# A graph network's third pass: the edge layer's first product in two PSUM banks, the adjacency windows in one

## The reference

```python
x = ln(x + L0(x))        # two max-aggregations with leaky relu: passes 1 and 2 over the edges
# L1, the third pass over the edges:
h = relu(edge_attr_17 @ W1.T + b1)          # "hidden", 96 wide, per edge
w = h @ W2.T + b2                           # "edge rows"
msg = w * x[src]                            # "message": x[src] is gathered
agg = segment_sum(msg, dst)                 # "sum"
x = ln(x + relu(x @ Ws.T + bs + agg @ Wn.T + bn))
x = ln(x + L2(x))        # two hops with a normalised adjacency matrix
x = ln(x + L3(x))        # one hop and a weight
```

## Time and profile before

| what | value |
|---|---|
| median of 3 runs | 4723.26 us (4720.13 to 4724.09) |
| the profiled execution | 4718.38 us |
| its span, first to last instruction | 4716.6 us |
| third pass, first hidden product to last message | 2561 to 3883 us |
| busy share of the span: PE, DVE, POOL, ACT | 75%, 53%, 50%, 20% |
| mean granted clock of TensorE | 0.843 |

### The profile page before, as it was taken

One profiled execution on the slowest core, in us unless ns is written; L12 is line 12 of the kernel. 1 busy time (PEld: TensorE's weight loads), 2 busy tenths in 40 slices (PEclk: granted clock), 3 DMA queues, 4 the chain that ended last, 5 costly groups with the idle time before them and its releaser, 6 DMA issues.

```text
span 4716.6 us, 64730 instructions
## 1 busy us (share of the span) xinstructions
PE 3549.1 (75%) x23472; PEld 2740.7 (58%) x23472; DVE 2500.2 (53%) x6368; ACT 929.8 (20%) x2714; POOL 2376.2 (50%) x2520
## 2 busy tenths in 40 slices
PE   3666776677647777777776676777777789999999
PEld 2444554454424544454444454555555569999999
DVE  4555666565636666666665455555555553232211
ACT  0100000000112222222222232332232230011100
POOL 5566666666466666666664566665565640000000
PEclk6788777777868888888887788878888889999999
DMA  5323232323223333333332222233333338777776
GB/s 148 100 63 73 63 73 65 72 62 73 60 66 104 97 102 98 101 102 106 97 103 67 68 78 70 76 90 93 105 105 103 103 98 267 275 255 257 257 275 241
DMA packets 192519, 555.56 MB, mean 118 GB/s; under 512 B 77782, under 2 KB 83382, under 8 KB 172662
## 3 DMA queue, kind: packets, MB, share of 16 engines
q1 hardware_dynamic: 67132, 335.46, 22.3%
q0 software_dynamic: 80432, 124.45, 12.8%
q10 hardware_dynamic: 44682, 92.08, 5.2%
HBM read 455.53 MB, written 96.37 MB: 117 GB/s over the span
## 4 chain that ended last, share of the span: by engine, by line
PE 46%; another core or an unknown queue 23%; DVE 14%; issue 9%; ACT 5%; ACTq 2%; DMA 1%; DVEq 0%; SPq 0%
PE banks L1443 17%; PE banks L1217 7%; PE banks L1173 5%; DVE scan L2293 5%; PE banks L1245 4%; DVE hot_key L2324 3%; PE banks L1170 3%; PE banks L1357 3%; PE banks L1189 3%; DVE hot_src L2326 2%; PE banks L1365 2%; ACT adj L1710 1%; DVE back L2298 1%; DVE hot_lo L1952 1%
## 5 line engine op out<-in xcount | busy, mean ns | idle before, releaser
L930 POOL DMA_INDIRECT gath<-table,ids x2496 | 2365.8, 948 | 1476.3 <-issue 687.2
L1217 PE MATMUL banks<-back 128*96 128x104 f32 (+11 forms) x6000 | 783.5, 279 | 180.3 <-issue 128.4
L1217 PEld LDWEIGHTS banks<-back 128*96 128x96 f32 x6000 | 721.5, 191 | 253.5 <-issue 185.3
L2324 DVE TENSOR_SCALAR hot_key<-banks,key_t 128x392 bf16<-128x392 int16 x1600 | 658.2, 411 | 315.2 <-remote 292.6
L1443 PE MATMUL banks<-r_parts,adj_in 128*128 128x288 bf16 x6543 | 809.6, 286 | 4.6 <-DMA adj_in<-adjacency 4.6
L1245 PE MATMUL banks<-hot_key,hot_src 128*128 128x392 bf16 x1600 | 459.1, 373 | 468.1 <-ACT adj L1710 292.5
L1443 PEld LDWEIGHTS banks<-r_parts,adj_in 128*128 128x128 bf16 x6543 | 802.4, 143 | 6.4 <-issue 4.4
L2293 DVE TENSOR_TENSOR_SCAN scan<-keep_of,scan,banks 96x512 f32<-96x512 bf16 x414 | 526.3, 1271 | 407.7 <-remote 320.5
L1245 PEld LDWEIGHTS banks<-hot_key,hot_src 128*128 128x128 bf16 x1600 | 149.3, 108 | 786.6 <-issue 726.0
L1173 PE MATMUL banks<-ea_of,w_edge_of 128*96 128x512 f32 x832 | 546.9, 742 | 18.3 <-issue 17.4
L1709 ACT ACTIVATE adj<-banks 128x160 bf16<-128x160 f32 x800 | 242.4, 303 | 1109.8 <-remote 720.3
(11 more groups left out here) (182 smaller groups left out, 2382.5 us busy)
## 6 DMA issues: line engine op xcount, KB each, us to landing
adj_in<-adjacency SPq DMA_DIRECT2D x114, 1568.0 KB, 6.5
adjacency<-adj ACTq DMA_DIRECT2D x100, 464.0 KB
gath<-table,ids POOLq DMA_INDIRECT x2496
ea_of<-in_ea_t SPq DMA_DIRECT2D x78, 512.0 KB
keep_of<-keep_max_d SPq DMA_DIRECT2D x52, 768.0 KB
adjacency<-adj ACTq DMA_DIRECT2D x100, 320.0 KB
adj_in<-adjacency SPq DMA_DIRECT2D x33, 928.0 KB, 4.8
ahead_of<-adjacency SPq DMA_DIRECT2D x33, 640.0 KB
```

What stands on the lines that cost most here:

```text
L930: pool.indirect_dma_start(gath[:, b, t, :], None, tables[p][:, :], bass.IndirectOffsetOnAxis(ap=ids[:, 1, n:n + 1], axis=0),).then_inc(s_g ...
L1217: m = pe.matmul(band_ps[g % 2][:, at:at + n], rows_in[:, q % 2, t * D:(t + 1) * D], hot_dst[:, q % 2, t, first:first + n], start=False, st ...
L2324: ve.tensor_scalar(hot_key[:, h, a, :], key_places_ps, key_t[:, 0, a, bass.ds(n, 1)], None, ALU.is_equal)
```

## The change

The hidden products of quarters 0 to 93 (`HID_PAIRED` = 94) alternate between banks 0 and 1, and each is issued in step `q-4`; `hidden(q)` then waits for the relu of quarter `q-2`. Before, all used bank 0, in step `q-3`, with a wait for the relu of `q-1`. From quarter 94 on bank, step and wait are as before. ACT reads the relu's input from the bank in question; its order of work is the same. To free bank 1, all 400 windows of the third pass now lie in bank 6: this moves 93 odd windows, those of the steps up to 93. In the second pass odd windows stay in bank 1. `hidden(1)` waits for the second pass's last window in bank 1, and the first `products_ahead` waits for the 94th relu, where it waited for bank 1's windows.

```diff
+HID_PAIRED = AHEAD_STEPS[0] // 2 * 2
...
-        hid1_ps = banks[0:D, 0, :]
+        hid2_ps = [banks[0:D, b, :] for b in (0, 1)]
...
         def window_bank(n):
-            step = (n - WINDOWS * BUILT) // 2 + 1
-            return 1 if n % 2 and step < AHEAD_STEPS[0] - 1 else 6
+            return 1 if n % 2 and n < WINDOWS * BUILT else 6
+        def hidden_bank(q):
+            return q % 2 if q < HID_PAIRED else 0
+        def hidden_step(q):
+            return q - (4 if q < HID_PAIRED else 3)
...
-                    if q >= 1:
+                    if q == 0:
+                        pe.wait_ge(s_copied[2], BANDS)
+                    elif q == 1:
+                        pe.wait_ge(s_window_out, windows_in(1, WINDOWS * NT))
+                    elif q < HID_PAIRED:
+                        pe.wait_ge(s_hid, q - 1)
+                    else:
                         pe.wait_ge(s_hid, q)
-                    else:
-                        pe.wait_ge(s_copied[2], BANDS)
-                    pe.matmul(hid1_ps, weights(2), columns, start=True, stop=True).then_inc(s_hid_ps, 1)
+                    pe.matmul(hid2_ps[hidden_bank(q)], weights(2), columns, start=True, stop=True).then_inc(s_hid_ps, 1)
...
-                            pe.wait_ge(s_window_out, windows_in(1, WINDOWS * NT))
+                            pe.wait_ge(s_hid, HID_PAIRED)
...
                 edge_rows(1)
+                hidden(3)
                 for s in range(QUARTERS + TAIL):
-                    if s + 3 < QUARTERS:
-                        hidden(s + 3)
+                    for q in (s + 3, s + 4):
+                        if q < QUARTERS and hidden_step(q) == s:
+                            hidden(q)
...
-                    act.activation(hid[0:D, q % 2, :], hid1_ps, ACT.Relu, bias=W["edge_in_b"][:, 0:1]).then_inc(s_hid, 1)
+                    act.activation(hid[0:D, q % 2, :], hid2_ps[hidden_bank(q)], ACT.Relu, bias=W["edge_in_b"][:, 0:1]).then_inc(s_hid, 1)
```

## The result

The changed kernel takes 4729.24 us (median of 16 runs), the kernel before 4723.7 us beside it (16 runs); the ratio is 1.0018, with a 95% interval of 1.0011 to 1.0024. That is some 8 us slower by the ratio and 5.5 us by the medians. One run of the changed kernel took 15243.89 us and is left out of the ratio. Predicted were 4735 us, a range of 4706 to 4752 us, and "slower by over 0.2%" as the likeliest case. The direction is right, and the time lies in the range. The likeliest case isn't shown, since 1.0018 is just under its bound and the interval lies on both sides of it.

What follows compares the result with a forecast made beforehand. POOL's gathers and pauses were taken to bound each step; one window bank would cost 12 us (between 6 and 16) and the other edits nothing, so 4723.3 + 12 = 4735 us, range 4706 to 4752 us.

Steps and rivals of the forecast that it cites:

- slower by over 0.2%: Whole kernel: the likeliest of three outcomes, chance 0.47, with its own range of 4732 to 4752 us.
- The forecast signs: First half: no relu wait at hidden products, windows' waits 64.0 towards 100 us, over 35 POOL pauses, step near 6.33 us.
- POOL's gathers and its share of a pause make a step.: Third pass: four gathers, 5.0 us, plus 1.25 or 1.46 us of pause make steps of 6.2 and 6.4 us.
- The removed wait for the relu is no gain, because PE stands at the windows instead.: Hidden products, first half: the removed 52.0 us of PE waiting mostly precede a stand at a window, so aren't saved.
- The faster rival: First half: the relu ends most runs ahead; removing it gives 31 pauses for 35, 12 us faster, 4711 us; chance 0.22.
- PE stops about half a step earlier in a silence.: Odd windows in bank 6: while ACT's and DVE's answers are missing, PE stops at the next window, half a step sooner.
- The sum, 12 us.: First half, 92 steps: loss taken as 12 us, between 6 us by an example and 16 us by the pauses.
- 2.1 quarters per pause: POOL, first half: 2.1 quarters instead of 2.4 between pauses of 3.0 us, 0.18 us a step, 16 us in all.
- the share of the early products: Second half's extra products: part of the 0.20 us step difference between halves; by an example 0.96 of 1.45 us.
- The one that could not be seen.: Third pass: PE's news seems to reach other engines late while gathers are in flight, and all at once when they pause.

Runs made afterwards that it cites:

- the second pair of traces: Both kernels unaltered, run and traced again: the changed kernel 4775.85 us, the kernel before 4769.72 us, ratio 1.0010.
- the runs with pauses: Kernel before, POOL made to wait for landed gathers in the third pass: before every third quarter 4240.65 us (repeat 4243.54), before every quarter 4563.44 us.

## Why the prediction was right in direction and too large in size

The forecast signs came: no wait of the hidden product for the relu, the windows' waits for ACT's copy up from 64.0 to 90.6 us, 41 pauses in place of 35, and a step of 6.25 us where 6.33 was forecast.

*POOL's gathers and its share of a pause make a step.* Held. The step grew by 0.05 us and the pauses by (113.1 - 105.0)/84 = 0.10 us a step, and the gaps under issue fell by 2.5 us (98.9 to 96.4).

*The removed wait for the relu is no gain, because PE stands at the windows instead.* Held, most clearly in the run with one window bank alone, where the relu's wait vanished by itself. The faster rival (0.22) needed the relu to end most of PE's runs ahead, and as a forecast for this change it fell. That the wait is worth nothing in every arrangement isn't shown: the run with another place in the step made it longer, and in the pair with one bank for the edge rows only 4.4 us of it were left.

*PE stops about half a step earlier in a silence.* Fits, by one timeline (2945.53) and by 154.0 us of idle time before windows; how many silences go that way wasn't counted. The second half's 1.48 us a step had been taken as the nearest row; after the change the first half has 154.0/84 = 1.83.

*The sum, 12 us.* The measured change is 5.5 us (medians) to 8 us (ratio), about half to two thirds of it. I had read 2.1 quarters per pause with pauses of 3.0 us. POOL got 84/41 = 2.05, but the mean pause was 113.1/41 = 2.76 us, as in the second half, and so the pauses cost 0.10 us a step more and not 0.18. That is the term that was mis-sized: more pauses, but each shorter. In the second pair of traces the pauses grew by only 0.9 us, so this split rests on one pair. For the share of the early products in the 0.20 us between the halves I had 0 and all as bounds and two thirds by an example. The run with one window bank alone has no early products in its first half: 6.30 us a step there and 663.5/104 = 6.38 in its own second half, which gives them 0.08 us of the 0.20. The changed kernel has 6.25 and 667.2/104 = 6.42, which gives 0.16. So their share stays open; it isn't nothing.

*The one that could not be seen.* The base of it all, that PE's news is late while gathers are in flight, was read from timelines and fits every trace here: remote waits in quarters 10 to 93 of 155 to 217 us on the chips of 4720 and 4770 us. No run tested it by an edit, since without gathers a chip of 4720 us wasn't tried. The kernel's own last 832 us speak for it: no gathers and no remote wait. The chip of 4040 us shows that gathers alone aren't enough. That these silences are what makes one window bank dear is argued from the waits and not shown. What ends a silence stays open as well.

## What to carry to other kernels

Before giving a product a second PSUM bank, count, for each bank choice, at which instruction TensorE stops when nothing comes back. Here one bank in place of two cost 0.15% for the windows and 0.40% for the edge rows; that the spare bank is best given to the product that stops TensorE first is a guess that fits, and no run tested it. A wait that a profile shows may be the one that comes first in a row of waits: here 52.0 us went away and 71 us appeared at the next product, and TensorE's whole idle time in that half stayed within 0.2 us of where it was. Where two halves of one pass differ in few respects, the second half is a cheap forecast for the first, but a count of pauses and their length are two numbers, and both have to be read from it.

## What the runs showed of the hardware that was not expected

The same kernel takes 4040, 4720 or 4770 us. The experiments' runs of 4040 us all carry chip number 6, those of 4720 and of 4770 us both carry number 5, so what sets these last two apart isn't known. On the first kind no trace has a remote wait of DVE for TensorE, neither in passes 1 and 2 nor in the third pass with all its gathers (the runs with pauses); on the others DVE waits 155 to 217 us in 84 steps for such updates, up to 9.2 us at a time, and several then come at once: after the silence shown, ACT goes on at 2888.14 and DVE at 2888.24 us. Passes 1 and 2 are slower there as well: the first message of the third pass comes at about 2176 us on the one and 2568 us on the other. A change that trades banks costs 0.2% where the kernel takes 4720 us and, without gathers, nothing that could be told on the other kind; what the whole changed kernel does on the chip of 4040 us wasn't run.
